# Rotary projection: halves exchanged by a ScalarE copy instead of a second product, values biased by a one-row product

## The reference, cut to what matters

```python
q = (x @ wq_w + wq_b).reshape(b, l, NH, HD)
k = (x @ wk_w + wk_b).reshape(b, l, NH, HD)
v = (x @ wv_w + wv_b).reshape(b, l, NH, HD)
# apply_rope on q and k, per head of 16:
first, second = jnp.split(inputs, 2, axis=-1)
out = jnp.concatenate([first * cos - second * sin, second * cos + first * sin], axis=-1)
```

## Time and profile before

| | |
|---|---|
| median of 3 runs | 1933.48 us (1928.55 to 1936.76) |
| profiled execution | 1935.03 us |
| its span | 1933.3 us |
| mean granted TensorE clock over the span | 0.815 |
| busy share PE, DVE, ACT, POOL | 75%, 75%, 44%, 31% |
| rotary projection | about 340 to 423 us of the span |

### The profile page before, as it was taken

The page is one execution under the profiler, slowest core; times in us unless marked ns, Lnnn a source line. Parts: engine busy times, 40 slices in busy tenths (PEclk is TensorE's granted clock), DMA queues, the critical chain, the costliest instruction groups (busy, mean ns, idle before and its releaser), DMA issues. The chain is left out here.

```text
span 1933.3 us, 35202 instructions
## 1 busy us (share of the span) xinstructions
PE 1459.6 (75%) x10462; PEld 857.0 (44%) x10463; DVE 1442.6 (75%) x4694; ACT 842.7 (44%) x2080; POOL 607.8 (31%) x1108
## 2 busy tenths in 40 slices
PE   7799898978888777999941777677677667666664
PEld 4232224544444454666620444554455444444553
DVE  4688885566777672111167999999999999899982
ACT  3366665224555522222212444455545554454432
POOL 3300000350000001111152445554555654455540
PEclk9799999888999977999965577667767777776767
DMA  6341230251222150111146002201030012200000
GB/s 170 98 166 49 62 88 1 61 129 40 62 53 49 76 230 28 46 46 43 44 147 160 17 21 57 54 7 26 13 92 18 10 28 59 71 2 12 1 1 13
DMA packets 73463, 113.51 MB, mean 59 GB/s; under 512 B 8750, under 2 KB 58842, under 8 KB 72540
## 3 DMA queue, kind: packets, MB, share of 16 engines
q1 hardware_dynamic: 69756, 102.22, 18.3%
q0 software_dynamic: 3552, 9.45, 1.8%
HBM read 74.11 MB, written 37.78 MB: 58 GB/s over the span
## 5 line engine op out<-in xcount | busy, mean ns | idle before, releaser
L1678 DVE MATCH_REPLACE8 top_left<-top_next,top_left 128x65 f32<-128x65 f32 (+15 forms) x768 | 322.0, 427 | 0.0
L1673 DVE MAX8 top_next<-top_left 128x8 f32<-128x65 f32 (+15 forms) x768 | 300.6, 432 | 0.0
L1133 POOL TENSOR_TENSOR top_e<-top_e,top_left 128x33 f32<-128x33 f32 (+3 forms) x254 | 188.5, 763 | 203.0 <-DVE top_left L1678 202.9
L1408 ACT ACTIVATE top_e<-top_ps_s,top_neg_max 128x129 f32<-128x129 f32 (+15 forms) x256 | 125.6, 491 | 192.5 <-POOL top_neg_max L1577 175.0
L742 DVE TENSOR_REDUCE tok_rowmax<-tok_ps_s 128x1 f32<-128x512 f32 x256 | 166.8, 688 | 29.2 <-PE tok_ps_s L584 26.5
L1251 PE MATMUL top_ps_pt<-ident,top_e 128*128 128x128 f32 x640 | 138.9, 346 | 26.0 <-issue 14.4
L2516 DVE TENSOR_TENSOR moe_hid<-moe_act_gate,moe_ps_h 128x512 f32<-128x512 f32 x39 | 26.8, 687 | 173.3 <-ACT moe_act_gate L2477 173.3
L742 DVE TENSOR_REDUCE rot_rowmax<-rot_ps_s 128x1 f32<-128x128 f32 (+3 forms) x256 | 115.6, 487 | 47.6 <-PE rot_ps_s L587 44.3
L715 ACT ACTIVATE tok_et<-tok_ps_st 128x1024 f32<-128x1024 f32 x128 | 124.2, 1021 | 51.2 <-PE tok_ps_st L618 51.1
L2416 PE MATMUL moe_ps_h<-moe_w,moe_rows_t 128*128 x312 | 143.1, 602 | 0.2 <-issue 0.2
L1420 ACT ACTIVATE top_prob_t<-top_ps_pt 128x128 f32<-128x128 f32 (+3 forms) x256 | 104.3, 431 | 67.7 <-PE top_ps_pt L1251 67.1
(11 more groups left out here) (375 smaller groups left out, 3227.9 us busy)
## 6 DMA issues: line engine op xcount, KB each, us to landing
moe_w<-in_moe_w SPq DMA_DIRECT2D x3, 4096.0 KB, 22.2
last_xs<-zeros SPq DMA_DIRECT2D x1, 5120.0 KB, 20.4
moe_ys<-moe_y SPq DMA_DIRECT2D x38, 128.0 KB, 1.8
top_vs<-v_by_position SPq DMA_DIRECT2D x16, 256.0 KB
k_parts<-rot_parts SPq DMA_DIRECT2D x16, 192.4 KB, 3.1
rot_ks<-k_parts SPq DMA_DIRECT2D x16, 192.4 KB
top_ks<-k_parts SPq DMA_DIRECT2D x16, 192.4 KB
q_parts<-tok_parts SPq DMA_DIRECT2D x16, 192.0 KB, 2.9
```

Source lines behind the costliest of these rows:

```text
L1133: eng.tensor_tensor(e[:, U % KEPT, 0:w], e[:, U % KEPT, 0:w], left[:, U % 4, 0:w], ALU.subtract).then_inc(prob_ok, 1)
L1408: act.activation(e[:, U % KEPT, 0:keys(U)], row(U), ACT.Exp, bias=neg_max[:, U % 4:U % 4 + 1]).then_inc(e_ok, 1)
L1673: dve.max(next8[:, U % 2, step // 2, :], left[:, U % 4, 0:keys(U)]).then_inc(pick, 1)
L1678: ins = dve.match_replace(left[:, U % 4, 0:w], next8[:, U % 2, step // 2 - 1, :], left[:, U % 4, 0:w], 0.0)
```

## The change

The weights' columns for queries and keys are put in another order, so that the first halves of all heads of a group pair lie in partitions 0 to 63 of the product and the second halves in 64 to 127. The second product `ps_rot` goes. ScalarE copies `ps` into `swapped` in two instructions that exchange the two partition halves, and VectorE's `turned` reads `swapped`. The values get their bias on TensorE by a product of one row of ones with the bias row, accumulated in `ps_v`, and ScalarE copies them to `va`. The stores take four DMAs of 32 partitions a step instead of two of 64. The addition of the residual bias moves from GpSimd's order in the projection to its order in the attention. The `tok` stages keep what they had (32 = two DMAs a step).

```diff
-STEP_STORES = 16 * 2
+HALF = HD * HG // 2
...
+            swapped = c.sbuf(st, f"{tag}_swapped", [P, 2, S], F32)
+            ones = c.sbuf(st, f"{tag}_ones", [1, P], F32)
...
-        ps_rot = c.psum(st, f"{tag}_ps_rot", [P, 2, S])
...
                     for i in range(2):
-                        sp.dma_start(dst[b, 2 * gg + i].rearrange("i d h t -> (d h) i t"),
-                                     parts[i * HD * HG:(i + 1) * HD * HG, :, k, span(k)]).then_inc(stored[k], 16)
+                        group = dst[b, 2 * gg + i].rearrange("i d h t -> (d h) i t")
+                        if rope:
+                            for half in range(2):
+                                sp.dma_start(group[half * HALF:(half + 1) * HALF],
+                                             parts[half * 2 * HALF + i * HALF:half * 2 * HALF + (i + 1) * HALF, :, k,
+                                                   span(k)]).then_inc(stored[k], 16)
...
                     for ch in range(DC):
                         mm = pe.matmul(ps[:, k % 2, :], ...)
-                    if rope:
-                        at = (3 + which) * D + gg * P
-                        for ch in range(DC):
-                            mm = pe.matmul(ps_rot[:, k % 2, :], w[:, ch, at:at + P],
-                                           c.xt[:, ch, b, 1:S + 1], start=ch == 0, stop=ch == DC - 1)
                     mm.then_inc(qk_mm, 1)
                     pe.wait_ge(v_ok, b * NQ + (k + 1))
                     for ch in range(DC):
                         mm = pe.matmul(ps_v[:, k % 2, 0:D], ...)
+                    if rope:
+                        if b == 0 and k == 0:
+                            pe.wait_ge(ones_ok, 1)
+                        mm = pe.matmul(ps_v[:, k % 2, 0:D], ones[:, :], vb[0:1, :], start=False, stop=True)
                     mm.then_inc(v_mm, 1)
...
                 dve.tensor_tensor(rest[:, k % 2, span(k)], ...)
+                if rope:
+                    return
...
                     if rope:
+                        dve.wait_ge(swap_ok, b * 8 + 2 * (k + 1))
                         dve.scalar_tensor_tensor(out=plain[:, k % 2, :], in0=ps[:, k % 2, :], ...)
-                        dve.scalar_tensor_tensor(out=turned[:, k % 2, :], in0=ps_rot[:, k % 2, :],
+                        dve.scalar_tensor_tensor(out=turned[:, k % 2, :], in0=swapped[:, k % 2, :],
...
+            def values(b, k):
+                n = b * NQ + k
+                if isinstance(b, int) and n == 0:
+                    act.wait_ge(v_ones, 2)
+                act.wait_ge(v_mm, n + 1)
+                act.activation(va[:, bass.ds(b, 1), :, k, :, 0:HD]...,
+                               ps_v[:, k % 2, 0:D]..., ACT.Copy).then_inc(v_ok, 1)
+
+            def exchange(b, k):
+                act.wait_ge(qk_mm, b * 4 + (k + 1))
+                act.wait_ge(full_ok, b * 4 + (k + 1))
+                for i in range(2):
+                    act.activation(swapped[i * (P // 2):(i + 1) * (P // 2), k % 2, :],
+                                   ps[P // 2 - i * (P // 2):P - i * (P // 2), k % 2, :], ACT.Copy).then_inc(swap_ok, 1)
+
             def image(b, before):
                 for k in range(4):
+                    if rope and k == 0:
+                        exchange(b, 0)
+                    if rope and k < 3:
+                        exchange(b, k + 1)
                     act.wait_ge(full_ok, b * 4 + (k + 3))
 
                     act.wait_ge(stored[k], b * step_stores + 16)
                     act.activation(hi[:, k, span(k)], full[:, k % 2, span(k)], ACT.Copy).then_inc(hi_ok, 1)
+                    if rope and k:
+                        values(b, k - 1)
+                    elif rope and before:
+                        values(b - 1, 3)
                     if k:
                         second_part(b, k - 1)
...
                     pool.tensor_tensor(lo[:, k, span(k)], ...)
-                    if bias is not None:
-                        h = c.h[:, bass.ds(b * NQ + k, 1), :].rearrange("p a n -> p (a n)")
-                        pool.tensor_tensor(h, h, bias[:, :], ALU.add)
...
                 pool.tensor_copy(vs[g][:, :, :], ...).then_inc(v_loaded[g], 1)
+                if bias is not None:
+                    pool.tensor_tensor(c.h[:, s, :], c.h[:, s, :], bias[:, :], ALU.add)
...
-    a["rot_w"] = _split_rows(np.concatenate([_by_place(wq), _by_place(wk), wv, turned_q, turned_k], axis=1))
+    a["rot_w"] = _split_rows(np.concatenate([_by_half(wq), _by_half(wk), wv], axis=1))
```

More of the change, by code:

```diff
@@ L199, with __init__ @@
 class Heads:
-    def __init__(self, c, stack, tag, width, ahead):
+    def __init__(self, c, stack, tag, width, ahead, step_stores=0):
         self.ahead = ahead
+        self.step_stores = step_stores
         if ahead > 1:
@@ L238, in load_step, with project @@
     load_keys(sp, c, b, g, k, loaded)
-def project(c, tag, w, qkb, vb, cls, heads, rope=None, first=False, bias=None):
+def project(c, tag, w, qkb, vb, cls, heads, rope=None, first=False):
     nc = c.nc
@@ L271, in project @@
         turn_ok = c.sem(st, f"{tag}_turn_ok")
+        swap_ok = c.sem(st, f"{tag}_swap_ok")
+        ones_ok = c.sem(st, f"{tag}_ones_ok")
         hi_ok = c.sem(st, f"{tag}_hi_ok")
@@ L279, in project @@
         v_ones = c.sem(st, f"{tag}_v_ones")
-        step_stores = STEP_STORES
+        step_stores = heads.step_stores
         fetched = 16 * c.fetches
@@ L344, in _ @@
                         mm = pe.matmul(ps_v[:, k % 2, 0:D], c.xt[:, ch, b, 1 + k * P:1 + k * P + P],
-                                       w[:, ch, 2 * D:3 * D], start=ch == 0, stop=ch == DC - 1)
+                                       w[:, ch, 2 * D:3 * D], start=ch == 0, stop=ch == DC - 1 and not rope)
+                    if rope:
+                        if b == 0 and k == 0:
+                            pe.wait_ge(ones_ok, 1)
+                        mm = pe.matmul(ps_v[:, k % 2, 0:D], ones[:, :], vb[0:1, :], start=False, stop=True)
                     mm.then_inc(v_mm, 1)
@@ L353, in _ @@
             dve.sem_inc(v_ok, 2)
+            if rope:
+                dve.memset(ones[:, :], 1.0).then_inc(ones_ok, 1)
             dve.wait_ge(c.fetched, fetched)
@@ L375, in split @@
                 n = b * NQ + k
-                if isinstance(b, int) and n == 0 and not first:
-                    dve.wait_ge(v_ones, 2)
+                if rope:
+                    return
                 dve.wait_ge(v_mm, n + 1)
@@ L439, in _ @@
                 image(b, True)
+            if rope:
+                values(B - 1, 3)
             second_part(B - 1, 3)
@@ L454, in _, with attend @@
                                        ALU.subtract).then_inc(lo_ok, 1)
-                    if bias is not None:
-                        h = c.h[:, bass.ds(b * NQ + k, 1), :].rearrange("p a n -> p (a n)")
-                        pool.tensor_tensor(h, h, bias[:, :], ALU.add)
-            if bias is not None:
-                pool.tensor_tensor(c.h[0:B, NT, :], c.h[0:B, NT, :], bias[0:B, :], ALU.add)
-def attend(c, tag, causal, heads, clear=False, fetch=()):
+def attend(c, tag, causal, heads, clear=False, fetch=(), bias=None):
     nc = c.nc
@@ L570, in _ @@
                                  ).then_inc(v_loaded[g], 1)
+                if bias is not None:
+                    pool.tensor_tensor(c.h[:, s, :], c.h[:, s, :], bias[:, :], ALU.add)
+            if bias is not None:
+                pool.tensor_tensor(c.h[0:B, NT, :], c.h[0:B, NT, :], bias[0:B, :], ALU.add)
         @block.tensor
@@ L3312, in program @@
                 with ExitStack() as near:
-                    heads = Heads(c, near, "rot", S + 1, 2)
-                    project(c, "rot", *w_rot, cls=True, heads=heads, rope=tables, bias=wo_rot[1])
-                    attend(c, "rot", causal=True, heads=heads)
+                    heads = Heads(c, near, "rot", S + 1, 2, 16 * 4)
+                    project(c, "rot", *w_rot, cls=True, heads=heads, rope=tables)
+                    attend(c, "rot", causal=True, heads=heads, bias=wo_rot[1])
             w13 = c.sbuf(moe, "moe_w13", [P, DC, E, 2 * MOE_HIDDEN], F32)
@@ L3380, in layout @@
     cos, sin = np.cos(angle).astype(np.float32), np.sin(angle).astype(np.float32)
-    a["cos"] = np.tile(np.repeat(np.concatenate([cos, cos]), HG, axis=0), (P // HD // HG, 1))
-    a["sin"] = np.tile(np.repeat(np.concatenate([-sin, sin]), HG, axis=0), (P // HD // HG, 1))
+    cos, sin = (np.tile(np.repeat(table, HG, axis=0), (P // HD // HG, 1)) for table in (cos, sin))
+    a["cos"], a["sin"] = np.concatenate([cos, cos]), np.concatenate([-sin, sin])
     a["top_w"] = _split_rows(np.concatenate([_by_place(i["L1_attn_Wq"].T), _by_place(i["L1_attn_Wk"].T),
```

18 lines of the change are left out of this document (12 added, 6 removed).

## The result

The changed kernel takes 1977.03 us (median of four runs, 1973.17 to 1980.14) against 1931.01 for the kernel before beside it: ratio 1.0239 [1.0218, 1.026], 46 us slower. The forecast was 1954, and 1969 the end of its range: the direction and the wait that was forecast came out, the size did not.

The account below looks back on a forecast made before the run. TensorE's matmul work was taken to bound the projection. With half its time at 1.2 GHz: +19.65 (steps) - 2.08 (start) + 3.2 (tail) = +20.8; 1935.03 + 20.8 - 1.55 = 1954 us, 8-in-10 range 1936 to 1969.

Parts of the forecast that it names:

- The loop and its wait: Rotary projection: PE's values wait for ScalarE's value copy two steps back, behind the exchange; 2.24 us in 10 of 15 intervals.
- The half copies: ScalarE's exchange in the projection: two copies between partition halves, 1.10 us together, part of PE's wait.
- PE's own work, 3.00 us a step: Projection step on PE: product 1.71, values 0.86 and one-row product 0.43 us, at full clock.
- I take half the time at 1.2 GHz (mean 0.75): Projection's clock, taken from the upper attention: 15 intervals take 84.1 us, 19.65 more than before.
- The rule of the Trainium skill weighed there: PE's clock stays up through short gaps between bursts; by it the projection holds full clock and the sum is +4.5 us.
- the rows of 1402 to 1404: Upper attention in the earlier profile: granted clock 0.69 after a PE wait of 2.09 us, cited against the clock holding.
- Start and tail: Projection's ends: the first product without the second behind it saves 2.08 us; later, more numerous stores at the end add 3.2.
- Late stores, a rival: Projection: four small stores a step delay ScalarE's high part, adding 14.3 us to the forecast, 1969; chance 0.07.
- The residual bias: nothing on the path: GpSimd's 17 additions, moved behind the attention's value copies, fit between them and cost nothing.
- had slack, so neither matters by itself: VectorE in the projection: losing the values' bias addition and waiting for the exchange copies cost nothing by themselves.

Follow-up runs that it names:

- g3: Changed kernel with values copied before the exchange, residual additions behind the attention's first four copies, exchanged halves in PSUM and a 128-row bias product: 1925.6 us.
- e2: Changed kernel with extra matmuls, read by nobody, filling PE's wait in each waiting step: 1953.8 us.
- f4: Changed kernel without the one-row product, so the values lack their bias: 1950.7 us.
- g1: Changed kernel with a 128-row bias product (one row of ones, the others zeros) in place of the one-row product: 1959.4 us.
- e3: Kernel before the change, with only the residual bias additions moved to GpSimd's order in the attention: 1941.6 us, ratio 1.0055.
- e1: Changed kernel with ScalarE's value copy of two steps back put ahead of the exchange: 1940.0 us.
- f2: Changed kernel with values copied before the exchange and all seventeen residual additions behind the attention's first four copies: 1933.4 us.
- e4: Changed kernel with VectorE adding the bias and copying the values as before, without one-row product or ScalarE value copy: 1937.4 us.

## Why the prediction was wrong, step by step

The spans are 45.1 us apart, and 20.8 were forecast. The 24.3 that are missing are, but for rounding, 17.6 between the first and the last product, 7.0 in the attention and its output, 1.4 elsewhere, less 0.8 each for the start and the tail.

**The loop and its wait: right.** 2.24 us were forecast; the trace has 2.22 (2.38 in the stream of matmuls: from the values of 350.37 to those of 356.15 are 5.78 us, less 3.40), eleven times, and free steps where they were expected. The half copies, forecast at 0.55, took 0.59; the value copy 0.36 as taken.

**PE's own work, 3.00 us a step: too small.** The one-row product was priced as "half of 0.86, 0.43 us", by its columns. It takes 0.63, and the free step 3.40. By columns it would have been right with 128 rows: g3 has 0.43 and 3.05. Over 15 steps this is 6.0 us at full clock. The price stood in the trace of the kernel before, whose upper attention has a product of the same shape; first at full clock, then at the low one:

```profile
1337.99 0.69 PE L1304 MATMUL top_ps_x<-top_vb,top_ones 1*128 1x256 f32 x2
1338.62 1.13 PE L1302 MATMUL top_ps_x<-top_w,top_next_xt 128*128 128x256 f32 x4
...
1405.50 1.22 PE L1304 MATMUL top_ps_x<-top_vb,top_ones 1*128 1x256 f32 x2
1406.65 1.11 PE L1251 MATMUL top_ps_pt<-ident,top_e 128*128 128x128 f32 x4
```

1338.62 - 1337.99 = 0.63 and 1406.65 - 1405.50 = 1.15, the 0.63 and 1.14 of the changed kernel.

**"I take half the time at 1.2 GHz (mean 0.75)": the step that failed most.** The stage ran at 0.68. Between the end of the first product and that of the last (346.97 to 448.62, the latter 0.20 ahead of ScalarE's exchange at 448.82) the 15 intervals took 101.65 us instead of 84.1, at a clock of 0.70. Of the 17.6 us missed, 1.4 are the wait (10 x 0.14), 6.0 the work, and the remaining 10.2 the clock: 26.9 us in place of 16.7. e2 confirms the size with 24.5. The parts depend on the order in which they are put right, since longer work is also doubled at the low clock: half the time at each level with the measured 5.78 and 3.40 gives 93.6 us, so 9.5 of the 17.6 go to the sizes and 8.0 to the clock. The rule of the Trainium skill weighed there (TensorE: Matmul & The Clock Gate, Why this matters for your kernels), by which gaps of this size pass, did not hold: 0.68 with gaps of 2.22 us, and 0.83 with the same gaps and no bias product (f4), as the rows of 1402 to 1404 had it. And 0.75, taken over from another stage, would have been too low with 128 rows (g1: 0.81) or without the product (f4: 0.83). What was overlooked is the one row, at both its prices: its own time and what it does to the clock.

**Start and tail: about right.** The start saves 2.9 instead of 2.1 us. The tail is 460.23 - 448.62 = 11.6 against 9.2, +2.4 instead of +3.2: eight stores were issued at 0.43 us each, not 0.61. Late stores, a rival, did not occur.

**"The residual bias: nothing on the path": wrong.** The additions lay where the prediction put them, and no wait on GpSimd arose. What was not asked is what runs on VectorE at that moment: 5.5 us over twelve strips of the 9.8 by which the attention grew, and 10 us of the whole in e3. In the rest the clock was lower too, 0.89 against 0.91 over the attention; how much of it that makes is not shown. The trace of before showed it in small: `rot_neg_sum`, 0.18 us by itself, took 0.40 to 0.52 in nine strips, beside the copies.

**VectorE "had slack, so neither matters by itself": right in the changed kernel**, where it waits for PE's clock, and hidden: with the loop gone, PE waits for `full` (4.9 us in e1, 5.2 in f2), which stands behind the two-input `turned`.

**Open.** The attention of e1 took 327.4 us against 312.7 in f2; the additions explain about 5 of them, its clock was 0.83 against 0.88, and why is not shown. e3's 10 us are also more than the 5.5 of its longer VectorE additions. What in a one-row product lowers the clock is open too.

## What to carry to other kernels

When work is moved to an engine that has time, look at what each order of instructions makes wait for what: a copy queued behind an exchange cost 37 us (1977.0 against 1940.0), and the same copy one place earlier makes no wait. A stop of TensorE that recurs can be paid a second time in clock (stops of 2.2 us were, e4's of up to 1.8 us were not in 360 to 400 us), so price it at both levels and ask what the matmuls around it look like. Before pricing an instruction in proportion to another, look in the trace for one of the same shape, the same rows included. Before moving a GpSimd instruction into "free" time, or an operand from PSUM to SBUF, look which VectorE instructions with two SBUF inputs lie beside it.

## What the runs showed of the hardware

- A float32 product of one row by 256 columns took 0.63 us at full clock and 1.14 at the low one; with 128 rows and the same columns 0.43 and 0.86 (g1). In a loop with equal stops of 2.2 us the granted clock was 0.68 with the one-row product, 0.81 with the 128-row one, 0.83 with none; in e4, with stops of 0.9 to 1.8 us in nearly every step and PE busy 27.67 of 40 us, it was 1.00 (360 to 400 us).
- VectorE's two-input operations took 0.64 instead of 0.175 us beside a GpSimd addition, and up to 1.62 instead of 0.74 beside `lo`; `turned` with one input in PSUM kept 0.74, and so did the row maxima out of PSUM their 0.49.
- A store of half the partitions was issued in 0.43 us instead of 0.61, so twice as many cost 1.4 times the queue time.
